# Reordering VectorE's reciprocals and GpSimd's low parts in an eight-head graph attention layer

## The reference

```python
Wh = (h @ W).reshape(b, n, H, HD).transpose(0, 2, 1, 3)      # H = 8, HD = 16
e1 = einsum('bhnd,d->bhn', Wh, a[:HD]); e2 = einsum('bhnd,d->bhn', Wh, a[HD:])
e = e1[:, :, :, None] + e2[:, :, None, :]
e = where(adj_mask[:, None] == 0, -inf, e)
e = where(e >= 0, e, 0.2 * e)
attn = softmax(e, axis=-1)
h_prime = einsum('bhij,bhjd->bhid', attn, Wh)
x = layernorm(x + h_prime)
```

## Time and profile before

| | us |
|---|---|
| median of 3 runs (lowest, highest) | 788.59 (786.36, 789.25) |
| profiled execution's own time | 786.59 |
| its span, first to last instruction | 781.4 |

### The profile page before, as it was taken

One profiled execution on the slowest core, in us unless ns is written; L12 is line 12 of the kernel. 1 busy time (PEld: TensorE's weight loads), 2 busy tenths in 40 slices (PEclk: granted clock), 3 DMA queues, 4 the chain that ended last, 5 costly groups with the idle time before them and its releaser, 6 DMA issues.

```text
span 781.4 us, 26071 instructions
## 1 busy us (share of the span) xinstructions
PE 697.0 (89%) x8484; PEld 513.6 (66%) x8484; DVE 616.6 (79%) x1786; ACT 555.6 (71%) x1270; POOL 399.0 (51%) x615
## 2 busy tenths in 40 slices
PE   5898999989998689989949999969999999999992
PEld 4566666666665467767738999936666666666661
DVE  2688788887888769999987888866787877778765
ACT  3565666656665489999848999837878777787871
POOL 5577778787787424454431111105546464555541
PEclk9999999999999799999969999969999999999996
DMA  6343333433322213322222333401222222222211
GB/s 170 83 104 73 96 92 76 101 70 98 86 44 43 27 15 36 39 34 34 34 54 55 87 89 81 88 1 21 57 48 54 49 52 60 45 56 47 56 49 42
DMA packets 34906, 47.75 MB, mean 61 GB/s; under 512 B 4388, under 2 KB 18472, under 8 KB 34856
## 3 DMA queue, kind: packets, MB, share of 16 engines
q0 software_dynamic: 18576, 21.01, 16.8%
q1 hardware_dynamic: 15992, 25.97, 10.9%
q10 hardware_dynamic: 288, 0.13, 0.1%
HBM read 51.32 MB, written 8.39 MB: 76 GB/s over the span
## 4 chain that ended last, share of the span: by engine, by line
PE 54%; DVE 25%; issue 9%; ACT 8%; DVEq 3%; DMA 0%; ACTq 0%; POOL 0%; SPq 0%; POOLq 0%
PE banks L1175 7%; DVE pp L573 7%; PE banks L1490 5%; PE banks L1501 4%; PE banks L1474 4%; PE banks L1516 4%; PE banks L1464 4%; PE banks L1469 4%; DVE pp L896 3%; PE banks L1508 3%; PE banks L1183 3%; PE banks L692 3%; DVE stats L585 3%; PE banks L1458 2%; DVE oo L907 2%
## 5 line engine op out<-in xcount | busy, mean ns | idle before, releaser
L573 DVE SCALAR_TENSOR_TENSOR pp<-banks,floor,adj 128x1024 f32<-128x1024 f32 x128 | 157.5, 1249 | 6.9 <-PE banks L679 4.4
L1258 POOL TENSOR_TENSOR pp<-pp,adj 128x512 f32<-128x512 f32 x64 | 73.3, 1162 | 135.0 <-ACT pp L1299 135.0
L490 ACT COPY rows<-banks 128x640 bf16<-128x640 bf16 x64 | 44.3, 692 | 67.0 <-PE banks L669 66.9
L1299 ACT ACTIVATE pp<-banks,nobound 128x512 f32<-128x512 f32 x128 | 81.4, 695 | 3.5 <-PE banks L1490 1.8
L692 PE MATMUL banks<-pp,yv 128*17 128x128 f32 x2048 | 82.4, 280 | 1.3 <-DVE pp L573 1.3
L798 POOL TENSOR_TENSOR yres<-oo,x 128x512 f32 (+1 forms) x32 | 40.8, 1276 | 69.0 <-DVE oo L914 69.0
L679 PE MATMUL banks<-rows 32*128 32x128 bf16 x1024 | 51.2, 219 | 20.4 <-DVE pp L573 18.7
L1175 PE MATMUL banks<-w2b,xt 128*128 128x256 f32 x256 | 62.3, 387 | 0.0
L409 POOL TENSOR_TENSOR yv<-wh,yv 128x512 f32<-128x512 f32 x32 | 35.1, 1098 | 46.6 <-ACT yv L483 46.6
L1036 POOL DMA_DIRECT2D adj<-in_adj x32 | 17.0, 531 | 80.4 <-ACT sq L1074 80.4
L495 ACT COPY ot<-banks 128x512 f32<-128x512 f32 x64 | 37.3, 583 | 28.4 <-PE banks L692 28.4
(11 more groups left out here) (208 smaller groups left out, 1938.3 us busy)
## 6 DMA issues: line engine op xcount, KB each, us to landing
adj<-in_adjt POOLq DMA_DIRECT2D x96, 128.0 KB, 3.0
xt<-in_xt SPq DMA_DIRECT2D x32, 256.0 KB, 3.8
x<-in_x SPq DMA_DIRECT2D x32, 256.0 KB, 3.2
adj<-in_adj POOLq DMA_DIRECT2D x32, 256.0 KB, 3.0
out_ngd<-yres SPq DMA_DIRECT2D x32, 256.0 KB, 2.0
ident<-in_ident ACTq DMA_DIRECT2D x1, 64.0 KB, 2.3
w0t<-in_w0t SPq DMA_DIRECT2D x1, 64.0 KB, 2.1
w0e<-in_w ACTq DMA_DIRECT2D x1, 64.0 KB, 2.3
```

The costliest lines, as they stand in the source:

```text
L490: nc.scalar.copy(rows[:, slot % 2, a, :], R[:, 0:5 * N]).then_inc(s["rw"], 1)
L573: nc.vector.scalar_tensor_tensor(pp[:, g], S[g % 2][:, :].rearrange("p (h n) -> p h n", n=N), floor[:, slot:slot + 1], adj[:, slot, g:g + ...
L1258: nc.gpsimd.tensor_tensor(pp[:, slot % 2, h], pp[:, slot % 2, h], adj[:, slot], ALU.mult).then_inc(s["pm"], 1)
L1299: nc.scalar.activation(pp[:, slot % 2, h], S[h][:, :], ACT.Exp, bias=k["nobound"][:, :], scale=SCALE).then_inc(s["p"], 1)
```

## The change

On VectorE the reciprocals of step t - 1 move from between the third and the fourth graph's weights to behind the fourth's. On GpSimd the four `low` instructions of step t + 2 move from behind `values(t + 1)` to in front of it. Nothing is added or removed.

```diff
@@ GpSimd, step @@
             if in2:
                 load_adj(t + 2, a2)
                 high(t + 2, a2)
+            if in2:
+                low(t + 2, a2)
             if not known(t) or t + 1 < T:
                 values(t + 1, a1)
-            if in2:
-                low(t + 2, a2)
             if not known(t) or t >= 1:
                 divide(t - 1, c0)
@@ VectorE, step @@
             weights(t, 2, slot, lap)
+            weights(t, 3, slot, lap)
             if not known(t) or t >= 1:
                 invert(t - 1, c0)
-            weights(t, 3, slot, lap)
             if not known(t) or t >= 2:
                 statistics(t - 2, c1)
```

## The result

| | before | after |
|---|---|---|
| median of 6 runs, us (lowest, highest) | 788.17 (786.36, 789.25) | 782.98 (780.9, 785.17) |
| ratio, 95% interval | | 0.9938 (0.992, 0.9957) |
| profiled execution, its span | 786.59, 781.4 | 782.31, 777.4 |

The change makes the kernel 4.9 us faster. The forecast was 779.8 us, a gain of 7.8 us. The sign and the range (774 to 786) held, but 782.98 lies just outside the 777 to 782.5 us that the forecast itself stood for, and some 3 us of the gain didn't come.

A forecast was written before the change was run, and what follows sets the result against it. VectorE's wait for ScalarE's `turned` copy, holding weights 3 behind the reciprocals, was taken as the bound; 3.5 us in the loop plus 4.3 at the end made 7.8, giving 779.8 us, range 774 to 786.

The forecast's parts named there:

- What bounded the loop, and the edit on VectorE: Loop steps: weights 3 fill VectorE's 1.28 us wait before the reciprocals, freeing 1.1 us; top_lanes then waits for `wh`.
- The sum of the new step: Loop: hidden, `wh` copy, release, weights 0, scores 2 sum to 7.26 to 7.38 us, against 7.44; gain 0.12 per step.
- rival 2: Loop: top_lanes' new wait delays weights 0 by 0.2 us, step 7.52 us; about 786.5 us, no difference; chance 0.13.
- The loop's 3.5 us: Six loop bodies of four steps, each gaining 0.22 + 3 x 0.12 us: 3.5 us (2.0 to 4.9).
- The idle time at the loop's end: VectorE's 0.43 us of idle time before weights 0, at the end of a loop body, was to stay.
- rival 3: VectorE and GpSimd hold each other up, weights 3 waiting out `values`; 1 to 2 us left, 787 us; chance 0.06.
- Steps 28 to 31, 4.3 us: Last steps, without top_lanes or hidden: weights 3 come off whole, four times 1.1 less 0.1, gaining 4.3 us.
- rival 5: Only the end gains, the loop's slack eaten by releases of 0.15 us and more: 4.3 us, 783.3 us; chance 0.10.
- GpSimd, nothing: GpSimd's low parts before `values`: `values` don't move, `divide` starts some 0.3 us earlier, nothing on the chain waits; priced nothing.
- Rival 1: TensorE becomes the loop's bound if the `wh` copy doesn't hold top_lanes: 16.5 us gained, 771.3 us; chance 0.06.
- Rival 4, the clock: Moved times drop a full-clock TensorE stretch to 1.2 GHz; slower from 12 us of such work; chance 0.05.
- The base: Start of the forecast: the middle between results from the profiled execution's 786.59 us and the runs' median, 788.59 us.

The follow-up runs named there:

- old-lanes run: Full change, but top_lanes reads the preceding step's `wh` copy, so it waits for nothing new (maxima not the intended ones); ratio 0.9788 to the kernel before, loop steps 7.05 us.
- hidden-first run: Full change, plus TensorE's second hidden before the second tiles and ScalarE's second `wh` copy before the second rows copy; ratio 0.985 to the kernel before.
- end-only run: Kernel before, with VectorE's reciprocals behind the fourth graph's weights in steps 28 to 31 alone, GpSimd unchanged; ratio 0.9938 to the kernel before.

## Why the prediction was right, and where it was not

- **What bounded the loop, and the edit on VectorE.** Right. Weights 3 moved into the idle time, the reciprocals did not move, VectorE was ready for top_lanes 1.1 us earlier, and the `wh` copy was next (0.88 us of idle time before top_lanes; 0.8 was named). The old-lanes run shows that this copy is the bound, the hidden-first run that moving it pays what it should.
- **The sum of the new step.** 4.53 to hidden, measured 112.39 - 107.86 = 4.53. 1.20 to the end of the copy, measured 113.59 - 112.39 = 1.20. The release, 0.03 to 0.15, was 0.02. Then 0.16 to weights 0: measured 0.35. This is the term that was mis-sized. It was read where VectorE was busy, when its queue had prepared the waits of weights 0 in part beforehand; once top_lanes itself waits, that work comes after it. Then 1.34 to scores 2, measured 1.34. With 0.35 the sum is 7.44, which is the old step to the hundredth. So loop steps of 7.26 to 7.38 us and a `normalize` 7 to 8 us earlier (3.6 by the two profiles) did not come, and the sign named for rival 2, weights 0 over 0.3 us behind top_lanes, did.
- **The loop's 3.5 us** thus became 0.5. Rival 2 had the mechanism and the size per step (0.2 us), with a chance of 0.13; where I argued against it, the 0.15 us at the reciprocals was taken as if it held all of that work. Its step of 7.52 us took the middle of my releases, 0.09; the release was 0.02 and the addition 0.19, which gives 7.44. The idle time at the loop's end, which I said stays, grew as well: top_lanes to weights 0 is 0.81 us there, where it was 97.94 - 97.31 = 0.63. The body is still 0.08 us shorter, so the loop loses nothing. Rival 2 was also mis-added: 1.9 us lost against 4.3 won is 785.2 us, not 786.5; and rival 3's 1 to 2 us of gain leave 785.6 to 786.6, not 787. The 0.16 us, the one distance that the rows gave, was read with the engine busy; it turned out too short for the engine idle, and I had put no upper bound beside it.
- **Steps 28 to 31, 4.3 us.** Right: 4.32 by the two traces, and the end-only run has the whole ratio, 0.9938. Two single profiles are thin ground for that, since the clock moves this stretch too: it takes 34.40 to 35.66 us in the four profiles with the old order there and 29.93 to 31.19 in the nine with the new one (the end-only run's is 31.19, with a granted clock of 0.64 from 20 to 24 us into the stretch, where the full change has 1.00). The means, 34.93 and 30.58, are 4.35 apart. What came true is thus the number of rival 5, only the end gains, 783.3 us against 782.98, with a chance of 0.10; not its reason, releases of 0.15 us and more, since the release was 0.02.
- **GpSimd, nothing.** Right, by its own run. `values` start 2.46 us behind scores 2 in both kernels, and wait less in the new order (12.2 us against 35.9 in the same waits view) only because low fills that time. `divide` starts 4.33 us behind scores 2 instead of 4.47, so 0.14 us earlier and not 0.3.
- **Rival 3, values and weights in each other's way.** It did not happen: they now run at once (`values` from 110.32 to 111.42 us, weights 1 to 3 from 107.92 to 111.56), `values` in 1.10 us and three weights in 3.64, 1.21 each, as before the change. No time is lost to anything the two engines share. The Trainium skill's GPSIMD Engine Reference ("Key points") names a collision only with VectorE instructions in a two-port mode or with two SBUF inputs, and weights, with one input in PSUM, are not among the latter; the trace agrees.
- **Rival 1** needs the copy out of the way, and the old-lanes run shows its world: by the waits, not TensorE alone but top_row through top_all is then the bound, at 7.05 us.
- **Rival 4, the clock.** It didn't come as a slower kernel. But it touched what is measured, in step 0, in the last steps, and once more (below), where the sign named for this rival, a clock under 0.9 between 30 and 240 us, appears in a profile of the unaltered changed kernel.
- **The base.** The middle between profiled time and median was 787.6 against a median of 788.17 in more runs.

With 4.3 + 0.5 = 4.8 us the corrected sum meets the measured 0.0062 x 788.17 = 4.9 us, whose interval goes from 3.4 to 6.3. That they agree to 0.1 us is luck: in the second set, at a granted clock of 0.960 to 0.963, the changed kernel's span (777.3 us, 3 executions) is 3.4 us under that of the kernel before (780.7, 4 executions), and at 0.959 or less 4.2 us.

## What to carry to other kernels

When an instruction moves into an idle time, ask what is late next, and take the distances on the new chain from places where that very instruction waits: a start-to-start distance read on a busy engine leaves out what its queue did in advance. In this kernel's hardware loop such work was 0.19 us at the wait that the change exposed (0.35 against 0.16). It was hidden behind a busy engine and laid bare behind an idle one, so swapping one wait for an equally long one can cost more than the slack between them. Steps at the ends of a pipeline, where a stage is absent, may carry the whole gain: price them apart from the loop.

## What was not expected of the hardware

- Writing out one engine's loop, the others unchanged, took 6.3 us off the kernel before and 7.9 off the changed one. The step with the loop's return alone became 0.64 us shorter, six times.
- In the first return of the loop TensorE now stands idle 1.12 us (0.89 before), and in two of the four profiles whose loop is that of the full change the clock then fell. In the stretch 72 to 78 us the granted clock was 1.00 in the first profile of the full change and 0.72 in the second (third number from the end):

```profile
72.00:78.00 6.00, 6.00 (x90) 4.48 (x89) 3.58 (x8) 3.86 (x10) 3.36 (x4) 0.72 0.20 58
```

The step takes 9.5 us instead of 7.98 then. None of the three profiles with the old order in the loop has it. Seven profiles don't show whether the longer idle time is the cause; this stays open.
